# A last expert layer whose blocks gather their rows: places from one-hot products, norm on three engines, unread products on TensorE

## What is computed

```python
logits = jnp.einsum('bsh,he->bse', x, w_router)        # 8 experts
probs = jax.nn.softmax(logits, axis=-1)
sel = jnp.argmax(probs, axis=-1)
wgt = jnp.take_along_axis(probs, sel[..., None], axis=-1)[..., 0]
for e in range(n_experts):
    h = jax.nn.relu(xt @ w1[e] + b1[e])                # 128 -> 512
    y = h @ w2[e] + b2[e]                              # 512 -> 128
    m = (sel_t == e).astype(xt.dtype) * wgt_t
    out = out + m[:, None] * y
```

## Time and profile before

| | us |
|---|---|
| median of 3 runs | 1015.03 (1013.06 to 1021.93) |
| the profiled execution, its own time | 1021.81 |
| its span, first to last instruction | 1020.0 |

### The profile page before, as it was taken

The page is one execution under the profiler, slowest core; times in us unless marked ns, Lnnn a source line. Parts: engine busy times, 40 slices in busy tenths (PEclk is TensorE's granted clock), DMA queues, the critical chain, the costliest instruction groups (busy, mean ns, idle before and its releaser), DMA issues. The chain is left out here.

```text
span 1020.0 us, 19335 instructions
## 1 busy us (share of the span) xinstructions
PE 913.1 (90%) x6140; PEld 606.8 (59%) x6140; DVE 734.7 (72%) x2087; ACT 643.6 (63%) x1433; POOL 536.6 (53%) x664
## 2 busy tenths in 40 slices
PE   7999989899999999989999999989998998963297
PEld 5444444444678888866556666656665755552297
DVE  6467777773889999877987978797887789444022
ACT  2456556654678888845867677767777766741175
POOL 4143726343704345102667867786768768941444
PEclk9689999985999999999999999999999978985599
DMA  4000001000443434130000000000000000001883
GB/s 137 1 1 1 22 2 44 1 23 2 125 140 117 132 111 105 40 120 1 2 1 2 1 2 2 2 1 2 2 1 2 2 1 1 2 1 47 280 295 101
DMA packets 31131, 47.73 MB, mean 47 GB/s; under 512 B 3805, under 2 KB 18674, under 8 KB 30913
## 3 DMA queue, kind: packets, MB, share of 16 engines
q1 hardware_dynamic: 29104, 43.42, 14.2%
q0 software_dynamic: 1504, 3.17, 0.8%
q10 hardware_dynamic: 432, 0.01, 0.0%
HBM read 40.25 MB, written 6.79 MB: 46 GB/s over the span
## 5 line engine op out<-in xcount | busy, mean ns | idle before, releaser
L1506 POOL TENSOR_SCALAR probs<-probs,rinv 128x128 f32<-128x128 f32 (+3 forms) x256 | 273.7, 1084 | 109.7 <-DVE rinv L1371 109.7
L1365 DVE CUSTOM_DVE_ANT_0 probs<-psum,adj 128x128 f32<-128x128 f32 (+3 forms) x256 | 122.2, 478 | 58.4 <-PE psum L1226 42.6
L1441 ACT ACTIVATE probs<-probs,rowmin 128x128 f32<-128x128 f32 (+3 forms) x256 | 141.7, 560 | 27.4 <-DVE rowmin L1365 26.2
L1450 ACT ACTIVATE pt<-psum 128x128 f32<-128x128 f32 (+3 forms) x256 | 98.4, 435 | 76.5 <-PE psum L1236 74.4
L841 ACT ACTIVATE pT<-psum 128x1024 f32<-128x1024 f32 (+3 forms) x128 | 89.6, 702 | 67.1 <-PE psum L597 66.1
L1226 PE MATMUL psum<-k_sb,q_sb 64*128 64x256 f32 (+3 forms) x512 | 112.9, 494 | 18.4 <-DVE rowmin L1365 17.8
L769 DVE TENSOR_REDUCE top<-psum 128x2 f32<-128x256 f32 (+3 forms) x128 | 102.7, 818 | 23.7 <-PE psum L577 23.4
L1354 DVE MAX8 top<-w 128x8 f32<-128x131 f32 (+3 forms) x208 | 103.2, 496 | 4.6
L1236 PEld LDWEIGHTS psum<-ident,probs 128*128 128x128 f32 x640 | 68.7, 142 | 59.6 <-POOL probs L1506 33.5
L1814 ACT ACTIVATE r_hid<-psum,b1t 128x512 f32<-128x512 f32 x125 | 82.6, 689 | 30.7 <-PE psum L1653 26.8
L900 POOL TENSOR_SCALAR_AFFINE_SELECT pT<-pT 128x512 f32<-128x512 f32 x64 | 40.9, 639 | 115.0 <-ACT pT L841 114.9
(11 more groups left out here) (306 smaller groups left out, 1886.2 us busy)
## 6 DMA issues: line engine op xcount, KB each, us to landing
r_share<-shares SPq DMA_DIRECT2D x12, 1024.0 KB, 7.1
s_wb<-in_w_all SPq DMA_DIRECT2D x23, 514.5 KB, 5.5
sorted_x<-blank SPq DMA_DIRECT2D x1, 2967.0 KB, 11.4
s_xg<-sorted_x SPq DMA_DIRECT2D x23, 129.0 KB, 2.5
r_w1s<-in_w SPq DMA_DIRECT2D x16, 128.0 KB, 5.7
r_w2s<-in_w SPq DMA_DIRECT2D x16, 128.0 KB, 6.2
r_share<-shares SPq DMA_DIRECT2D x6, 256.0 KB, 3.5
r_share<-shares SPq DMA_DIRECT2D x2, 768.0 KB, 5.0
```

Of the source, the lines that this page charges most:

```text
L1365: dve.tensor_tensor_reduce(probs[:, k, 0:K], s_bank[h][:, 0:K], adj[:, OFF[i]:OFF[i] + K], 1.0, FLOOR, ALU.add, ALU.min, rowmin[:, k:k + 1 ...
L1441: act.activation(probs[:, k, 0:K], probs[:, k, 0:K], ACT.Exp, bias=rowmin[:, k:k + 1], scale=-1.0, accum_out=rsum[:, k:k + 1]).then_inc(ex ...
L1450: act.activation(pt[:, (2 * n + h) % 4, 0:K], t_bank[h][:, 0:K], ACT.Copy).then_inc(pt_ready, 1)
L1506: pool.tensor_scalar(probs[:, k, 0:K], probs[:, k, 0:K], rinv[:, k:k + 1], None, ALU.mult).then_inc(normed, 1)
```

## The change

- The third layer no longer fills `sorted_x`, and the two memsets of its blank row at the start of the program are gone. Instead VectorE takes the means and variances of a batch's four tiles for the last layer in the next batch's steps 16 and 18 (`dve_stats_last`): 12 of the 16 tiles.
- The last layer's norm: ScalarE takes the root of 12 tiles at once; group 2 is normed by VectorE, group 0 by ScalarE (as scale and shift), group 1 by GpSimd, group 3 by VectorE after its own means. TensorE takes them in the order 2, 0, 1, 3.
- `pe_warm` is called with 20 products at the start of the layer, 4 behind the turning of each group, 10 ahead of the counts, 36 behind them, and 40 ahead of the first block.
- Choice: the largest logit, the shifted logits, then 8 - e where the logit is the largest, the maximum of that, and `sel` where it is equal. The weight of the chosen expert is 1 / (sum of exponentials).
- Places: no scatter. SyncE stores `x_tok` and `pay` (normed x and weight, 129 columns) in token order to a table `rows_x` in DRAM. VectorE splits each token's place into block and slot and makes two bf16 factors: `hot` (slot one-hot, 128 x 128 for each tile) and `part` (for each block the token's row number and tile number, 46 columns). TensorE's 16 products of them, summed in one PSUM bank, give for each slot of each block the token's number. Two more steps make from it the list to gather by and the list to scatter by.
- GpSimd makes the blocks' table itself, and then gathers each block's rows from `rows_x` with an indirect DMA: 12 blocks ahead, the other 11 one behind each scatter to the output. `sp_fetch` is gone; `OD` is 6.

```diff
@@ attention1
-                    @block.sync
-                    def _(sp):
-                        sp.dma_start(sorted_x[:, :].rearrange("(n p) w -> p n w", p=P),
-                                     blank[:].unsqueeze(1).to_broadcast([P, SLOTS_L1 // P, 2 * C + 2])).then_inc(vacant, 16)
@@ dve_program of attention1
+                        if n < NS and n // SLOTS1 and n % SLOTS1 in (16, 18):
+                            dve_stats_last(dve, late, n // SLOTS1 - 1, n % SLOTS1 // 18)
@@ pe_program
+                    pe_warm(pe, banks[0], 20)
+                    for p in range(CH + 1):
+                        if p < CH:
+                            pe.wait_ge(xn_ready[ORDER[p]], 1)
...
+                            pe_warm(pe, banks[0], 4)
...
+                    pe_warm(pe, banks[0], 10)
                     pe.wait_ge(chosen, 1)
                     flat = sel[:].rearrange("p t e -> p (t e)")
                     pe.matmul(banks[4][:, 0:T * E], strict[:], flat, start=True, stop=True)
                     pe.matmul(banks[3][:, 0:T * E], ones[:], flat, start=True, stop=True).then_inc(prefixes, 1)
+                    pe_warm(pe, banks[0], 36)
+
+                    for t in range(T):
+                        pe.wait_ge(hot_ready, t + 2)
+                        mm = pe.matmul(banks[2][:, 0:2 * NBLK], hot[:, t, :], part[:, t].rearrange("p a b -> p (a b)"),
+                                       start=(t == 0), stop=(t == T - 1))
+                    mm.then_inc(indexed, 1)
+                    pe_warm(pe, banks[0], 40)
                     pe_turn(pe, 0)
@@ dve_places, behind destf
+                    D.count(dve.tensor_copy(dest[:], destf[:]).then_inc(router_step, 1))
...
+                    D.count(dve.tensor_scalar(dest[:], dest[:], BLK - 1, None, ALU.bitwise_and).then_inc(router_step, 1))
...
+                    D.count(dve.tensor_copy(slot[:], dest[:]).then_inc(router_step, 1))
...
+                    D.count(dve.tensor_tensor(blk_of[:], destf[:], slot[:], ALU.subtract).then_inc(router_step, 1))
...
+                    D.count(dve.tensor_tensor(there[:], blk_of[:].unsqueeze(2).to_broadcast([P, T, NBLK]),
+                                              blk_at[:].unsqueeze(1).to_broadcast([P, T, NBLK]),
+                                              ALU.is_equal).then_inc(router_step, 1))
...
+                    D.count(dve.tensor_scalar(part[:, :, 0, :], there[:], row_no[:, 0:1], None,
+                                              ALU.mult).then_inc(router_step, 1))
+                    dve.tensor_tensor(part[:, :, 1, :], there[:], tile_no[:].unsqueeze(2).to_broadcast([P, T, NBLK]),
+                                      ALU.mult).then_inc(hot_ready, 1)
+                    for t in range(T):
+                        dve.tensor_scalar(hot[:, t, :], slot_no[:], slot[:, t:t + 1], None,
+                                          ALU.is_equal).then_inc(hot_ready, 1)
@@ pool_program
+                    pool.wait_ge(stored, 32)
+                    pool.wait_ge(take_ready, 1)
+                    for b in range(AHEAD):
+                        pool_take(pool, b)
                     for b in range(NBLK):
                         pool_put(pool, b)
+                        if b + AHEAD < NBLK:
+                            pool_take(pool, b + AHEAD)
@@ sp_program
+                    at_rows = rows_x[:, :].rearrange("(t p) w -> p t w", p=P)
+                    sp.dma_start(at_rows[:, :, 0:C], x_tok[:]).then_inc(stored, 16)
+                    for q in range(CH):
+                        sp.wait_ge(xn_ready[q], 1)
+                    sp.wait_ge(weighted, 1)
+                    sp.dma_start(at_rows[:, :, C:W], pay[:]).then_inc(stored, 16)
                     sp.wait_ge(table_ready, 1)
...
                     for b in range(NBLK):
-                        sp_fetch(sp, b)
-                    for b in range(WD, NBLK):
                         sp_weights(sp, b)
```

More of the change, by code:

```diff
@@ L29 @@
 SENTINEL = 1e37
-NOWHERE = 1 << 30
+NOWHERE = 4096.0
 LEAD = 33
-NCONST = 14
+NCONST = 12
 def apart(eng, passed):
@@ L1371, in dve_invert, with dve_stats_last @@
                     dve.reciprocal(rinv[:, k:k + 2], rsum[:, k:k + 2]).then_inc(inverted, 1)
+                def dve_stats_last(dve, late, b, part):
+                    for t in range(b * NT, (b + 1) * NT):
+                        if part == 0:
+                            late.count(dve.bn_stats(st[:, t, :], x_tok[:, t, :]).then_inc(late_step, 1))
+                        else:
+                            if t == b * NT:
+                                dve.wait_ge(late_step, late.done())
+                            late.count(dve.bn_aggr(mv_last[:, t, :], st[:, t, :]).then_inc(late_step, 1))
+                    if part:
+                        dve.wait_ge(late_step, late.done())
+                        ts = slice(b * NT, (b + 1) * NT)
+                        dve.tensor_scalar(ve_last[:, ts], mv_last[:, ts, 1], EPS, None, ALU.add)
                 def dve_program(dve):
+                    late = Steps(0, 2 * NT * (B - 1))
                     for i in range(NT):
@@ new lines, in dve_places @@
+                    dve.wait_ge(indexed, 1)
+                    made = banks[2][:, 0:2 * NBLK].rearrange("p (a b) -> p a b", a=2)
+                    D.count(dve.tensor_copy(token[:], made[:, 0, :]).then_inc(router_step, 1))
+                    dve.wait_ge(router_step, D.done())
+                    D.count(dve.scalar_tensor_tensor(out=token[:], in0=made[:, 1, :], scalar=float(P), in1=token[:],
+                                                     op0=ALU.mult, op1=ALU.add).then_inc(router_step, 1))
@@ new lines, in dve_places @@
+                    dve.wait_ge(router_step, D.done())
+                    dve.tensor_scalar(take[:], token[:], -1.0, 0.0, ALU.add, ALU.max).then_inc(take_ready, 1)
+                    D.count(dve.tensor_scalar(nobody[:], token[:], 0.0, NOWHERE, ALU.is_equal,
+                                              ALU.mult).then_inc(router_step, 1))
+                    dve.wait_ge(router_step, D.done())
+                    dve.scalar_tensor_tensor(out=give[:], in0=token[:], scalar=-1.0, in1=nobody[:],
+                                             op0=ALU.add, op1=ALU.add).then_inc(give_ready, 1)
@@ new lines, in pool_program @@
+                    half = E // 2
+                    for k in range(3):
+                        pool.wait_ge(table_step, k + 2)
+                        pool.tensor_tensor(before_b[:, :, 0:half], before_b[:, :, 0:half], before_b[:, :, half:2 * half],
+                                           ALU.add).then_inc(table_step, 1)
+                        half //= 2
+                    pool.wait_ge(table_step, 5)
+                    pool.tensor_scalar(table[:], before_b[:, :, 0], float(E - 1), None, ALU.min).then_inc(table_ready, 1)
```

268 lines of the change are left out of this document (134 added, 134 removed).

## The result

| | us |
|---|---|
| kernel before, median of 20 runs beside it | 1017.49 (1010.01 to 1022.89) |
| changed kernel, median of 20 runs | 1025.76 (1021.17 to 1033.1) |
| ratio | 1.0079, 95% interval 1.0062 to 1.0096 |
| its profiled execution's span | 1025.0 |

Slower by 0.8%, where 996.0 (988 to 1005) was predicted. Further down the same kernel, unaltered, takes 998.54 on another chip: both numbers are part of the result, and most of this text is about what lies between them.

What follows compares the result with a forecast made beforehand. The last layer's serial head, with sixteen GpSimd scatters, and TensorE's pace in the body were taken as the bound; -21.5 there and +2.2 in attention gave -19.3 from 1015.03, so 996 us, range 988 to 1005.

Steps and rivals of the forecast that it cites:

- Parts 1 and 2: Last layer's norm and router end 3.0 us earlier; with choice and counts, places start 7.8 earlier, at 924.4.
- rival of a falling clock: TensorE's clock falls in the router's part despite unread products: about +7 us, time 1003; chance 20%.
- Part 3: Last layer's places: `hot` tiles take 4.2 us, and the list to gather by is there at 935.7.
- Part 4: Gather instead of scatter: rows at 943.3, 40 unread products end at 944.0 and start the body, -17.4 us so far.
- 4.4: Start of the last layer's body: block 2's products come 4.4 us after the first turn at 2.4 GHz, before 7.06.
- Part 5: Last layer's body starts at full clock; GpSimd's row of 46 issues ends last; span ends at 998.5, -21.5 us with the head.
- -2.7: Saving in us from the body's first blocks running at 2.4 GHz instead of 1.2 GHz.
- Part 6: Third layer's attention: added means and variances in VectorE's queue cost +2.2 us (bounds 0 and 4.2).
- GpSimd's queue is slower: Gathers cost GpSimd more than 1.26 us each; nothing gained at 2.1, over 1% slower (1025) from 2.5; chance 4%.
- Block 0's rows land late: Block 0's gather lands late behind 4 MB of weights, body starts 5 us later, about 1001; chance 4%.
- Attention1 loses more: VectorE's lag in the third layer's batch 3 lengthens TensorE's gaps: +4 us, about 1000; chance 10%.
- -19.3: Forecast total in us for the whole kernel: -21.5 in the last layer and +2.2 in the third layer's attention.

Runs made afterwards that it cites:

- again: The changed kernel without any edit, run on another chip (chip 5) beside the kernel before: 998.54 us, ratio 0.9824 to the kernel before.
- lead3: Changed kernel, but GpSimd issues three gathers, then the other nine ahead only once block 0 is copied: 1017.38 us, ratio 1.0012 to the kernel before.
- all23: Changed kernel with all 23 gathers issued in one row ahead of the first scatter: 1024.78 us, ratio 1.0074 to the kernel before.
- pool_plain: Changed kernel with each gather replaced by a plain DMA of 128 rows in order from GpSimd's queue: 999.85 us, ratio 0.9806 to the kernel before.
- sorted: Changed kernel's head up to the places, then the kernel before's row scatter and plain fetches, with 20 unread products: 1009.75 us, ratio 0.9932 to the kernel before.
- best: Changed kernel with 1032-byte rows, own rows for unowned slots, and 24 unread products instead of 40: 1018.14 us, ratio 1.0004 to the kernel before.
- in_order: Changed kernel gathering by a fixed list in row order (0, 1, 2, ..., modulo 2048): 999.85 us, ratio 0.9821 to the kernel before.

## Why the prediction was wrong, by its own steps

Times from the layer's start: 908.1 in the forecast, 907.40 in the first profile, 905.10 in again.

| step | forecast | first profile | again |
|---|---|---|---|
| router's end | 13.4 | 13.4 | 13.4 |
| counts end, places start | 16.3 | 16.2 | 16.2 |
| first gather's issue | 28.5 | 28.1 | 28.1 |
| first turn | 35.9 | 35.4 | 35.4 |
| its copy | | 45.35 | 35.7 |
| last scatter's start | 85.9 | 112.5 | 86.2 |
| end of the span | 90.4 | 117.6 | 91.2 |

- **Parts 1 and 2** held to 0.1. The clock stayed at full through the router's part. The rival of a falling clock did not come. With unread products between the transposes, none of the 34 us of the two stretches above lost the clock (granted 1.00). By the rule of the Trainium skill (TensorE: Matmul & The Clock Gate, "Part 4: PE-mode transpose") the transposes don't count as busy. No run here has this part without the unread products, so none put the rule to the test.
- **Part 3**: the list came 0.4 earlier than forecast. The `hot` tiles took, grouped by line,

```profile
L2257 DVE TENSOR_SCALAR s_hot<-s_slot_no,s_slot 128x128 bf16<-128x128 f32 x16 | 3.2, 274 | 0.0
```

  3.2 for sixteen, 0.20 each, where the sum had 4.2. The Trainium skill (VectorE: DVE Perf Modes, "The perf-mode tier table") gives `tensor_scalar` on fp32 in SBUF two columns a cycle, from which the prediction's estimate was 2.1. The measured value lies halfway. The neighbouring steps ate most of the difference.
- **Part 4 is the step that failed**, and in a place where it had no term. It had the issue (0.95 and 0.30 between: right), the landing (in time: right), the 40 products (right), and then wrote "they, not the gather, start the body". Between TensorE's turn and its first products stands VectorE's copy. The ordinary hand-over to it was inside the 4.4 taken over from the earlier trace rows; that gathers under way could delay it was put at nothing. In the first profile it took 9.97 from start to start instead of 0.31. On chip 1 lead3, all23 and pool_plain tie this to the gathers by a list: three gathers ahead leave the first hand-over alone, 23 hold the second to 966.79, plain transfers of the same bytes hold up none. Why it happens on some chips and not on others is open.
- **Part 5** holds in again: 46 issues in one row, GpSimd ending last, two sums that waited for a buffer. On the halting chips the clock that -2.7 had counted on was lost again with the first halt, and hand-overs of the body are late too: of the 26.4 us between 117.6 and 91.2, 9.7 lie ahead of the first copy and 16.7 behind it.
- **Part 6** put +2.2 on the third layer, and the traces show 3.3. These are the first product of scores and the last products of the layer, before and in the first profile:

```profile
455.80 0.89 PE L1193 MATMUL psum<-k_sb,q_sb 64*128 64x128 f32 x4 [0.20 <-ACT k_sb L1433]
...
905.40 2.02 PE L1214 MATMUL psum<-wo,yt 128*128 128x128 f32 x16 [0.79 <-ACT yt L1457]
```

```profile
451.79 0.89 PE L1191 MATMUL psum<-k_sb,q_sb 64*128 64x128 f32 x4 [0.20 <-ACT k_sb L1448]
...
904.73 2.02 PE L1212 MATMUL psum<-wo,yt 128*128 128x128 f32 x16 [0.79 <-ACT yt L1472]
```

  That is 451.6 before and 455.0 after; the eighteen traces of the other runs have 454.5 to 455.0, sorted among them, which fills `sorted_x` in this layer as before. Of the kernel before there is one trace. Of the 3.3, 0.5 and 0.45 lie in batches 1 and 2, where 0.5 each was forecast, and 2.4 in batch 3, where 1.2 was. The place was right and the size in batch 3 half of what came. The start of the last layer (903.1 to 911.5 in these kernels) moves by more than this with the time of the layers ahead and doesn't show it.
- **Rivals.** None of them was this one. "GpSimd's queue is slower" came nearest in the sum (1025) and was wrong in its mechanism: issues took 1.25. "Block 0's rows land late" fell with TensorE's turn at 942.78. "Attention1 loses more" came in part, by 1.1. The forecast of the change's own work, -19.3, was near where nothing halts: 998.54 against 1015.86 on chip 5 is -17.3. The traces add up to it: the last layer takes 111.9 before and 91.2 in again, -20.7, and the third 3.2 more, -17.5 together. The fault was to take the same list DMA in the other direction, which the trace had only with the engines idle or one in 2.0 us, for proof that a row of gathers costs its neighbours nothing.

Two ways out were seen. **sorted** has no gather, costs 11 us against the changed kernel where that doesn't halt (0.9932 against 0.9824), and has only what the kernel before has, whose time is the same on all five chips; it was not run on a halting chip. Fewer gathers ahead help a little there: lead3 is 0.6% better than all23. best is 0.5 to 1.1% better than the other three on its chip with the same twelve gathers ahead; which of its three edits does it wasn't tried. Neither beats the kernel before.

## What to carry to other kernels

Where the profile shows an engine waiting for a neighbour that has long done its work ("remote", "issue", "another core"), the hand-over itself is late: look for what else is under way, here a row of DMAs that read by a list, and compare the record of the semaphore with the ends of the work on both sides. An experiment group needs the unaltered changed kernel in it; without that, six kernels on two chips "confirmed" a cure that was only another chip. A DMA by a list ahead of dependent work is to be priced on several chips before it is kept.

## What the runs showed of the hardware that was not expected

- The same kernel took 1025.76 in one place and 998.54 in another, while the kernel before stayed within 1015.9 to 1018.9 on five chips.
- In some places hand-overs from TensorE to VectorE or ScalarE take up to 12.9 us from start to start (all23, 941.26 to 954.13) while gathers by a list are under way; hand-overs to TensorE stay within 0.15 of the end of the work. In the first profile the late part is TensorE's addition to its semaphore (9.68). Scatters by a list, one every 2.0 us or three of them 1.28 apart at the end, don't do it. Why, and what in a gather by a list does it, is open.
- In the same places the last layer's traces lack 172 to 659 of 1136 landing records, and those of the other chips 5 to 14.
- 128 rows of 1028 bytes scattered by a list with 896 of 2944 writes to one row fill the DMA engines (share 1.25 at 104 GB/s), and weights of 514.5 KB take 12.6 us to land, where they take 5.6 in in_order on the same chip. Repeated row and row length are not told apart.
- Twelve means and variances put into VectorE's queue of the third layer (1.4 us of work in each of three batches) lengthen it by 3.3, of which 2.4 lie in the batch where TensorE already waits for VectorE.
- A VectorE compare of 128 fp32 columns against one number per row, written as bf16, takes 0.20 in a row of sixteen, not 0.26 as the norm's subtract and multiply.
